# An edge aggregation and its attention work dealt in quarters of a step, group sums added half a step later, and a routing stage in another order

## What is computed

```python
xn = _layernorm(x)
x = x + gnn(xn, edges) + attention(xn)       # part 1 and 2
x = x + moe(_layernorm(x))                   # part 3
# gnn: out = segment_sum(h[src] * dinv[src] * dinv[dst], dst) with h = xn @ W and a self loop;
#      out is normalised by ONE mean and standard deviation over all nodes, then PReLU
# attention: linear attention, 4 heads of 32: keys exp(k - max over nodes), context = sum k v,
#      queries soft-maxed per head, out = rmsnorm(q @ context @ w_out + b_out) + xn
# moe: 8 experts, the two best per node, gelu(x W1 + b1) W2 + b2, weighted sum of the two
```

## Time and profile before

| | us |
|---|---|
| median of 3 runs (lowest, highest) | 1724.48 (1723.1, 1737.27) |
| the profiled execution, own time | 1733.87 |
| its span | 1732.1 |

### The profile page before, as it was taken

The page is one execution under the profiler, slowest core; times in us unless marked ns, Lnnn a source line. Parts: engine busy times, 40 slices in busy tenths (PEclk is TensorE's granted clock), DMA queues, the critical chain, the costliest instruction groups (busy, mean ns, idle before and its releaser), DMA issues. The chain is left out here.

```text
span 1732.1 us, 31385 instructions
## 1 busy us (share of the span) xinstructions
PE 1330.6 (77%) x8996; PEld 1182.0 (68%) x8997; DVE 974.4 (56%) x2698; ACT 451.6 (26%) x1315; POOL 762.6 (44%) x838
## 2 busy tenths in 40 slices
PE   1895476677767788888778778994889999999930
PEld 1773466666667787877778767663379999999920
DVE  3998465555556767666677359788322222222237
ACT  1656200011112223223321110335423332323300
POOL 2002665555555556565566530333045555555510
PEclk9999687698988899999989899996589999999965
DMA  6004322222234455556567640005257666676648
GB/s 193 1 0 150 105 84 81 81 81 71 77 105 140 140 149 165 149 165 182 179 215 246 204 126 1 1 1 218 76 178 215 207 214 209 209 214 209 210 166 317
DMA packets 139994, 248.30 MB, mean 143 GB/s; under 512 B 20138, under 2 KB 96420, under 8 KB 139636
## 3 DMA queue, kind: packets, MB, share of 16 engines
q1 hardware_dynamic: 96568, 146.12, 26.9%
q0 software_dynamic: 34320, 93.76, 18.0%
q10 hardware_dynamic: 9004, 7.21, 1.3%
HBM read 213.65 MB, written 33.36 MB: 143 GB/s over the span
## 5 line engine op out<-in xcount | busy, mean ns | idle before, releaser
L712 POOL DMA_INDIRECT RG<-table,srci x504 | 483.2, 959 | 356.0 <-PE ps L729 186.3
L729 PEld LDWEIGHTS ps<-S_t,RG 128*128 128x128 f32 x2016 | 271.8, 214 | 5.7 <-issue 1.3
L729 PE MATMUL ps<-S_t,RG 128*128 128x96 f32 x2016 | 273.7, 295 | 1.3 <-DMA RG<-table,srci 0.7
L755 PE MATMUL ps<-R,zrow 128*128 128x128 f32 x1372 | 200.0, 288 | 19.8 <-DMA zrow<-table 16.0
L1806 PE MATMUL ps<-R,RG 128*128 128x128 f32 x1680 | 207.3, 277 | 0.0
L755 PEld LDWEIGHTS ps<-R,zrow 128*128 128x128 f32 x1372 | 188.9, 202 | 26.0 <-DMA zrow<-table 19.7
L1864 DVE TENSOR_TENSOR R<-ps,R 128x256 f32<-128x256 f32 x105 | 44.6, 425 | 278.9 <-PE ps L1816 271.1
L1816 PE MATMUL ps<-R 128*128 x840 | 198.5, 379 | 0.0
L1806 PEld LDWEIGHTS ps<-R,RG 128*128 128x128 f32 x1680 | 198.5, 194 | 0.0
L1839 ACT ACTIVATE R<-ps,RG 128x128 f32<-128x128 f32 x420 | 119.7, 368 | 279.0 <-PE ps L1806 263.7
L1890 POOL DMA_INDIRECT results<-R,S_t x105 | 103.6, 987 | 163.9 <-DVE R L1864 160.7
(11 more groups left out here) (355 smaller groups left out, 1983.9 us busy)
## 6 DMA issues: line engine op xcount, KB each, us to landing
RG<-in_w SPq DMA_DIRECT2D x106, 514.0 KB
zrow<-table SPq DMA_DIRECT2D x168, 256.0 KB
R<-results SPq DMA_DIRECT2D x48, 256.0 KB, 12.5
RG<-table,srci POOLq DMA_INDIRECT x504
table<-RG SPq DMA_DIRECT2D x12, 512.0 KB, 2.9
table<-R SPq DMA_DIRECT2D x12, 512.0 KB, 2.9
out<-R ACTq DMA_DIRECT2D x48, 128.0 KB, 5.9
R<-in_x SPq DMA_DIRECT2D x6, 896.0 KB
```

Of the source, the lines that this page charges most:

```text
L712: nc.gpsimd.indirect_dma_start(out=grows[:, s, :], out_offset=None, in_=table, in_offset=bass.IndirectOffsetOnAxis(ap=srci[:, ND + q, c:c ...
L729: last = nc.tensor.matmul(window(q % 2)[:, h, :], grows[:, s, h * P:(h + 1) * P], S_t[:, q % 2, c, :], start=c == 0, stop=c == GC - 1)
L755: last = nc.tensor.matmul(psD[:, h * P:(h + 1) * P], zrow[0:n, i % 3, s, h * P:(h + 1) * P], adj[b % 2][0:n, j, :], start=False, stop=False)
```

## The change

- Every share of a step is dealt in four quarters r = 0 to 3 on TensorE, ScalarE and VectorE. TensorE does the first half of features of `aggregate(q)` after quarter 1 and the second after quarter 3, and signals `pe_done` after the second as before.
- VectorE does `add(q-1)` after quarter 1 of step q in place of ahead of all, and `onehots(q+1)` after quarter 2. `add_block` stays at the head of the step, for one group fewer.
- The bounds move: keys in steps 0 to 15 (16 steps, before 23), keys and values in 18 to 44 (27, before 20), queries in 48 to 99 (52, before 50), the residual in 102 to 125 (24, before 26).
- In the third phase the joining of statistics of tile s-4 stands ahead of `finish(s-2)`. The ring `n_rows` has four sets in place of two, and 34 tiles of `norm` are ahead of the first `own_rows`, one follows after each round and eight after the last. POOL's search of the expert ids is gone; VectorE does it in three operations on one partition after the first round of `place`.

```diff
-        A0, A1 = 0, 23
-        C0, C1 = 25, 45
-        B0, B1 = 48, 98
-        D0, D1 = 100, GQ
+        A0, A1 = 0, 16
+        C0, C1 = 18, 45
+        B0, B1 = 48, 100
+        D0, D1 = 102, GQ
+        def quarter(seq, r):
+            seq = list(seq)
+            return seq[(len(seq) * r + 2) // 4:(len(seq) * (r + 1) + 2) // 4]
...
                 for q in range(GQ):                                   # TensorE
-                    some, more = list(chunks(q)), list(products(q))
-                    for n in range(max(len(some), len(more))):
-                        if n < len(some):
-                            count(some[n])
-                        if n < len(more):
-                            product(*more[n])
-                    attention(q)
-                    aggregate(q)
+                    for r in range(4):
+                        for m in quarter(chunks(q), r):
+                            count(m)
+                        for b, j in quarter(products(q), r):
+                            product(b, j)
+                        attention(q, r)
+                        if r % 2 == 1:
+                            aggregate(q, r // 2)
...
                 for q in range(GQ):                                   # VectorE
-                    if q >= 1:
-                        add(q - 1, blocks)
                     if q in USED[1:]:
-                        add_block(blocks, q)
+                        add_block(blocks, q - 1)
                         blocks += 1
-                    if q + 1 < GQ:
-                        onehots(q + 1)
-                    for m in chunks(q):
-                        chunk_add(m)
-                        if m + 3 < MD:
-                            chunk_onehots(m + 3)
-                    attention(q)
+                    for r in range(4):
+                        for m in quarter(chunks(q), r):
+                            chunk_add(m)
+                            if m + 3 < MD:
+                                chunk_onehots(m + 3)
+                        attention(q, r)
+                        if r == 1 and q >= 1:
+                            add(q - 1, blocks)
+                        if r == 2 and q + 1 < GQ:
+                            onehots(q + 1)
...
-            keep = [semaphore(phase, f"r_n_kept{k}") for k in range(2)]
+            keep = [semaphore(phase, f"r_n_kept{k}") for k in range(NR)]      # NR = 4
...
-                early = T - 2 * NROUND + 1
+                early = 34
...
-                    for t in range(early + 2 * r, min(early + 2 * r + 2, T)):
-                        norm(t)
+                    norm(early + r)
+                for t in range(early + NROUND, T):
+                    norm(t)
...
-                for e in range(NX - 1):                               # POOL
-                    nc.gpsimd.tensor_scalar(mask, steps, cumt[:, e:e + 1], None, ALU.is_ge).then_inc(pl, 1)
...
-                    nc.gpsimd.tensor_tensor(eidf, eidf, mask, ALU.add).then_inc(pl, 1)
...
                     if 0 <= s - 3 < T:
                         x_stats(s - 3)
+                    if 0 <= s - 4 < T:
+                        x_stats_joined(s - 4)
                     if 0 <= s - 2 < T:
                         finish(s - 2)
-                    if 0 <= s - 4 < T:
-                        x_stats_joined(s - 4)
...
                 for r in range(NROUND):                               # VectorE
                     place(r)
+                    if r == 0:
+                        ch.done(nc.vector.tensor_tensor(past, iwin[0:1, 0:NSTEP].unsqueeze(2).to_broadcast([1, NSTEP, NX - 1]),
+                                                        cumt[0:1, 0:NX - 1].unsqueeze(1)
+                                                        .to_broadcast([1, NSTEP, NX - 1]), ALU.is_ge))
+                        ch.done(nc.vector.tensor_reduce(eidf, past, AX.X, ALU.add))
+                        nc.vector.tensor_copy(eid_i, eidf).then_inc(eid_ok, 1)
```

More of the change, by code:

```diff
@@ L718, in _, with aggregate @@
             def _(pe):
[L719 to L731, removed]
+                def aggregate(q, h):
+                    if h == 0:
+                        pe.wait_ge(s_ok, q + 1)
+                        if q >= 2:
+                            pe.wait_ge(acc_ok, q - 1)
+                    for c in range(GC):
+                        s = 4 * ((q + FIRST) % 4) + c
+                        if h == 0:
+                            pe.wait_ge(got[s], (q // 4) * 16 + 16)
+                        last = nc.tensor.matmul(window(q % 2)[:, h, :], grows[:, s, h * P:(h + 1) * P],
+                                                S_t[:, q % 2, c, :], start=c == 0, stop=c == GC - 1)
+                    if h == KC - 1:
+                        last.then_inc(pe_done, 1)
                 def count(m):
@@ L821, in attention @@
                                          skip_group_check=True)
-                    for s in share(q, C0, C1, T + 1):
+                    for s in quarter(share(q, C0, C1, T + 1), r):
                         if s < T:
@@ L833, in attention @@
                         pe.wait_ge(mid_dve, 6)
-                    for s in share(q, B0, B1, T + 3):
+                    for s in quarter(share(q, B0, B1, T + 3), r):
                         if s < T:
@@ L1035, in residual, with attention @@
                     nc.vector.tensor_tensor(o_tile(t), o_tile(t), halved(xring[t % XR]), ALU.add).then_inc(res_ok, 1)
-                def attention(q):
-                    for t in share(q, A0, A1, T):
+                def attention(q, r):
+                    for t in quarter(share(q, A0, A1, T), r):
                         keys_max(t)
-                    if q == A1:
+                    if q == A1 and r == 2:
                         v.wait_ge(k_max, T)
@@ L1057, in attention @@
                         v.sem_inc(mid_dve, 1)
-                    for s in share(q, C0, C1, T + 1):
+                    for s in quarter(share(q, C0, C1, T + 1), r):
                         if s < T:
                             keys_less_max(s)
-                    if q == C1:
+                    if q == C1 and r == 2:
                         v.wait_ge(cx_ok, T)
@@ L1106, in attention @@
                                                                ALU.mult))
-                    for t in share(q, D0, D1, T):
+                    for t in quarter(share(q, D0, D1, T), r):
                         attention_norm(t)
```

108 lines of the change are left out of this document (52 added, 56 removed).

## The result

| | before | changed |
|---|---|---|
| median of 4 runs, us (lowest, highest) | 1727.13 (1723.1, 1737.27) | 1675.55 (1666.66, 1680.02) |
| ratio, 95% interval | | 0.9686 [0.9625, 0.9748] |
| the profiled execution: own time; span | 1733.87; 1732.1 | 1680.02; 1678.3 |

The change is 3.1% faster, 54 us between the profiled executions and 52 between the medians. The prediction said 1650 in a range from 1592 to 1717; of its 74 us, 54 came.

A forecast was written before the change was run, and what follows sets the result against it. The prediction took the step to be bound by a chain between engines and a gather loop of 6.15 us, no engine being full. Steps -67 and routing -7 made -74, giving 1650 us, range 1592 to 1717.

The forecast's parts named there:

- The floor of 6.15: Aggregation: a set of four gathers takes 5.0 us plus 1.15 for TensorE's signal, so no step is shorter than 6.15.
- the late signal: Aggregation: TensorE's signal can become visible 1.43 us after the matmuls' recorded end, or 0.14; possibly an error of the record.
- price of the steps: Aggregation: queries -24, residual -9, keys and values -22, keys -12 (at 5.9 us a step), together -67 us.
- steps of 5.65 us: Aggregation: the gather loop nearly broken, 5.65 us a step, taken into the low end of the range, 1592.
- The sum half a step later: VectorE's step: about 2.2 us of chunks and attention ahead of the sum cover nearly all the idle time before it.
- the halves: TensorE's aggregation: eight matmuls of 1.92 us become two fours of 0.96; taken as 0, bounds 0 and 0.14 a step.
- 22 us of keys and values: Part with keys and values: tiles fall from 2.5 to 1.85 a step, steps from 7.09 to 6.1 us, -22 us.
- Routing: Third phase: 16 norm tiles go before the first wait, so `own_rows` and the rounds start earlier; gain 7 us, bounds 2 to 8.
- Residual loop: Third phase: joining statistics ahead of `finish` swaps two operations of one engine; 0, bounds -5 and +5 us.
- Rival 1: Aggregation: the gather loop breaks and steps fall to TensorE's work, about 5.4 us, giving 1565; chance 0.12.
- Rival 2: Aggregation: waits return at the hand-offs, each VectorE quarter waiting; only routing is gained, 1717; chance 0.14.
- Rival 3: TensorE's clock falls to 0.73 with queries and residual, +75 us, 1800; decides from a clock of 0.85; chance 0.07.

The follow-up runs named there:

- experiment 6: The change with rows loaded by SyncE (consecutive rows, hardware DMA queue) and no GpSimd gathers; 1517.38 us against 1737.93 for the kernel before, ratio 0.8721.
- experiment 7: The change with each gather taking 64 bytes of a row in place of 1 KB; 1681.28 us, ratio 0.9663 to the kernel before.
- experiment 8: The change with one GpSimd operation and a wait for its end between the second and third gather; 1684.17 us, ratio 0.968 to the kernel before.
- experiment 3: The kernel before with only VectorE's step dealt in quarters, its sum and one-hots later, old bounds; 1591.32 us, ratio 0.9882.
- experiment 9: The kernel before with only VectorE's order changed, run again to meet held signals but on the unheld chip; 1591.98 us, ratio 0.9882.
- experiment 10: The change with VectorE's sum and one-hots back at the head of the step; 1547.24 us, ratio 0.9612 to the kernel before.
- experiment 5: The change itself, unaltered, run again beside the kernel before; 1683.59 us against 1737.93, ratio 0.9677.
- experiment 1: The kernel before with only the aggregation's changes (quarters, later sum, new bounds), old third phase; 1551.75 us against 1608.66, ratio 0.965.
- experiment 2: The kernel before with only the third phase's changes, old aggregation; 1599.84 us against 1608.66, ratio 0.9944.
- experiment 4: The change with the old bounds of the parts; 1541.09 us, ratio 0.9575 to the kernel before.
- experiment 11: The change with GpSimd waiting for TensorE every second step, then issuing eight gathers; 1540.69 us, ratio 0.9584 to the kernel before.
- experiment 12: The change with the old bounds, run again to see held signals; 1541.41 us, ratio 0.9581 to the kernel before.

## Why the prediction was right, and where it was not

**The floor of 6.15.** This was the step on which the sum rested, and it held: sets of gathers start 6.07 us apart in the median (71 of 121 are within 0.13 of 6.0), the steps average 6.24. It is where the steps settle and no hard bound: 14 of the 121 are under 5.85. The prediction took the late signal for something real at a place in GpSimd's rhythm; experiments 6 to 8 show that it is, and that it goes with GpSimd's gathers, not with their bytes or with TensorE alone. Of the rule of the Trainium skill (Perfetto Trace Analysis, Tensor Engine Instruction), that a matmul's end is an estimate and its semaphore is pushed later, this much is seen here: where nothing is held the signal follows the record's end within 0.02 us, and in the earlier trace rows VectorE acts 0.14 us behind it; a delay of up to 4 us is no error of the record, as seven signals of matmuls spread over 4 us arrive together, three engines act on them, and 168 us go when the gathers leave GpSimd.

**The size: 54 for 74.** The step of the prediction that fell short is its price of the steps, 67 us; measured are 48.5 (822.6 less 774.1), where its own steps over the new parts make 65. Of the 20 us missing in all, three lie ahead of the first of the 124 intervals, which starts at 204.6 for 201.7. The rest, 17, is in the steps. With keys they take 6.14 for the forecast 5.9, 4 us: 5.9 had been picked between two bounds, below the prediction's own floor of 6.15, and the loop holds there as well. With queries 6.30 for 6.15, 8 us, and with the residual 6.33 for 6.15, 5 us: the loop was counted for GpSimd alone, but SyncE sends for the rows `zrow` on TensorE's signals too. TensorE's idle time before the products, for those transfers, went from 19.8 to 40.8 us; in the unheld trace it is 17.9. That link is read from the traces; no run took it away by itself. With keys and values 6.10 stands against 6.1. Most sets start at the floor; what lifts the mean above the median of 6.07 are the long intervals, 30 of 121 over 6.5 us. One sum of the prediction is a little off: its steps of 5.65 us give 1596 for the low end of the range, not 1592.

**The sum half a step later.** The prediction gave all of the gain to it and put the halves at zero. Experiments 3, 9 and 10 say otherwise where signals are not held: of 55 us that the aggregation gains there (717.3 to 662.1), VectorE's order alone brings 8 to 14, everything but the later sum and one-hots 48. Put the other way, TensorE's and ScalarE's dealing (with the bounds) adds 42 to 47 to VectorE's, and the later sum adds 7 to the rest. The mechanism was named too narrowly. My reading is that the engines took turns because TensorE did its aggregation in one piece behind everything else, so that neither counts nor the end of the step came early; moving VectorE's wait alone gained with keys and values, lost with queries, and let half of the wait come back before the counts. How the 45.6 us divide with held signals is open: experiment 9 was meant for that and did not meet them.

**The bounds of the parts.** The 22 us of keys and values were reasoned from fewer tiles a step. With nothing held the old bounds give the same time twice (0.958 and 0.958 against 0.960). The gain in that part is the dealing's: 6.98 us a step in the old order, 5.06 in the change with the old bounds, over the same steps 23 to 45. With held signals the old bounds weren't seen.

**Routing.** 7 us forecast, 30.47 to 23.34 from first norm to first matmul in the traces, 9 us (6 to 12) by itself. **Residual loop:** zero, forecast zero: its 49 tiles take 93.6 us from first to last `shifted`, 93.4 before.

**The rivals.** Rival 1, steps at 5.4 us, did not happen in the run predicted, and is what the other chip shows (5.25). Rival 2's sign is in the trace, 192.7 us before the chunk adds, but the waits are the held signals', most ended by "remote" or late counts, and the steps did shorten. Rival 3: the clock rose with keys (0.73 to 0.83) and queries (0.93 to 0.95) and fell to 0.90 with keys and values (from 0.94) and 0.91 with the residual (from 0.93); the prediction's sign of being right, 0.93 or above, is met with queries only, but the 0.85 at which it decides is not reached. The Trainium skill (TensorE: Matmul & The Clock Gate, "A second HAM failure mode") ties a clock that goes back and forth to brief pauses between groups of matmuls. The traces agree at the ends: 0.99 to 1.00 in the sixth experiment, where TensorE is busy 94 to 98% with keys and values and with queries, 0.73 in the part with keys of the kernel before. Between them busy time doesn't order the clock: with keys and values it was 0.94 at 75% busy before and is 0.90 at 79% in the change, and with the residual 0.97 at 81% in the sixth experiment and 0.91 at 80% in the change. Why it fell in these two parts is open.

What stays open: why TensorE's signals are held on one chip while GpSimd issues gathers and not on another, with gathers of equal length (976 and 974 ns) in both; what it is in GpSimd's gathers that holds them; and whether eight gathers behind one wait gain or lose where they are held.

## What to carry to other kernels

When several engines stop waiting in the same instant for different matmuls, look for what holds the signals, not for what computes too slowly: here the instant follows the last of a burst of gathers by about a microsecond, and the burst plus that microsecond is what most steps settle at. Where nothing was held, dealing the engine that is waited for into pieces was worth more than moving the wait of the engine that waits, half of which came back at the next hand-off. And a gain of this kind is to be measured as a ratio within one chip, since the kernel before alone differs by 129 us between two.

## What the runs showed of the hardware

- While GpSimd issued indirect DMAs back to back (0.95 us each, 0.30 apart), TensorE's signals reached the others up to 4 us late and in clusters, mostly 0.8 to 1.6 us behind the last issue of four, in the first result and in experiments 5 and 7, and mostly 0.6 to 1.0 behind it in experiment 8. On the chip of experiments 1 to 4 and 9 to 12 they came within 0.02 us of the matmuls' recorded ends (experiment 1), and 7% of them behind a fourth gather rather than 63% (7 to 9% in the other runs with the work dealt on all engines, 16 to 17% in experiments 2, 3 and 9).
- The same kernel before takes 1609.3 us on the one chip and 1737.9 on the other. The old order's aggregation, 717.3 us unheld (experiment 2) and 845.7 held (the first result), makes up 128 us, that is all of it.
- The delay did not depend on the bytes gathered (64 or 1024 bytes a row: an aggregation of 803.5 and 804.1 us), and went with GpSimd's gathers (636.5).
- An operation of GpSimd that is no DMA, 0.59 us in the middle of a set, was free there (1684.17 us for 1683.59).
